# A position-wise expert mixture: 64 positions a stationary, half-width units, a block-diagonal bias product, two kinds of banks and a fetch on two queues

## The chip, the core and the metric

The kernel runs on one core of a Trainium2 chip. The metric is the device time of one execution in microseconds. The core's engines run side by side and meet through semaphores: TensorE (PE in the rows, its weight loads PEld), VectorE (DVE), ScalarE (ACT), GpSimd (POOL) and SyncE (SP, which here only issues DMAs).

## What is computed

The program is a chain of twelve stages of a perceiver over x, 32 batches of 64 positions of 256 columns, all float32: cross attention, attention and a feed-forward part, four times. The change is in the first feed-forward part, a mixture of eight experts whose gates belong to a position, not to a token. Cut to what matters:

```python
h = relu(x_normed @ gW1.T + gb1)             # per token
gate = mean_over_batch(h) @ gW2.T + gb2      # (64 positions, 8 experts)
W1 = einsum('se,eoi->soi', gate, eW1)        # a weight for each position
b1 = gate @ eb1
hid = relu(einsum('bsi,soi->bso', x_normed, W1) + b1)
W2 = einsum('se,edo->sdo', gate, eW2)
b2 = gate @ eb2
x = x + einsum('bso,sdo->bsd', hid, W2) + b2
```

The hidden width is 1024. So for each of 64 positions a 256x1024 and a 1024x256 weight are mixed from eight, and each is then applied to the 32 tokens (one per batch) of its position.

## The kernel before

x is resident in SBUF (16 tiles of 128 tokens), and its normed transpose XNT is written in the order of positions by the layernorm ahead (`layernorm_transposed`, which also issues the weight loads of the stage on SP and may run a `prepare` on GpSimd). `mixed_experts` computes the gates: two matrix products, a mean over the batch, and then, on VectorE, GB (the gates in blocks of 32 rows: four outputs by eight experts, masked so that one matmul with 32 rows mixes four outputs of every position) and GR (the gates repeated for the 32 batches, 2048 columns).

`position_experts` works through 16 units k: eight hidden blocks of 128 columns (k // 2), each for two halves of the positions (k % 2). GpSimd puts the loaded weights into expert-last order (`reorder1`, `reorder2`), TensorE turns them with transposes (T1, T2, 16 each), and the jobs of a unit are then, in TensorE's hand-written order: four mixing jobs f0 to f3 for the second weight (W2M), two first products A0 and A1 (each a bias product of four matmuls over `gates(...)` and EB1, then 32 matmuls over XNT and W1M), eight flips FL of the hidden rows, two second products Y0 and Y1 (16 matmuls over HT and W2M), and four mixing jobs g0 to g3 for the next unit's first weight (W1M). A mixing job is 16 matmuls: a stationary of 32 rows and 128 columns of the turned weight, a moving operand of 128 columns of GB (32 positions by four outputs), over four row groups of TensorE. Every job writes one of two buffers of four banks, in turn; `claim` lets job j wait until all that empties job j - 2 is done. Mixing and turning jobs are emptied half by ScalarE and half by VectorE (two copies of 512 columns each), hidden rows by ScalarE, second products by VectorE, which adds them up in Y. The turned second weight W2L has two buffers.

At the end SP stores Y for each half of the positions to DRAM, fetches it back in token order into YX, and VectorE adds it to x in four pieces.

All program semaphores that a stage has given up wait in a list; at the end of a stage, when it holds 64 or more, they are cleared and all engines meet at one more barrier.

## Time and profile before

| | |
|---|---|
| median of 3 runs | 2790.12 us (2789.54 to 2791.2) |
| profiled execution | 2791.36 us, span of its profile 2789.5 us |
| TensorE busy | 2520.1 us (90%) |
| VectorE, ScalarE, GpSimd busy | 1698.8 (61%), 1389.9 (50%), 730.5 us (26%) |
| the stage of the mixture | from 452.2 us (first turn) to 830.3 us (next stage starts) |
| the same, busy in it | TensorE 332.0, VectorE 233.8, ScalarE 181.7 us of 378 |

The profile gives start and length of every instruction; runs of equal ones stand in one row with their count and the idle time ahead of them, and what ended it. It has two entries for each float32 matmul of the program, and one for each transpose. A matmul's length includes the time in which its last columns drain, so the length of a job is read better from its start to the next job's start.

### The profile page before, as it was taken

The numbers are of one execution on the slowest core, as the hardware profiler recorded it, in microseconds if no ns is written. First come the engines' busy times: TensorE is split into PE (matmuls) and PEld (weight loads), VectorE is DVE, ScalarE is ACT, GpSimd is POOL, SyncE is SP. The second block draws the span as 40 slices with busy tenths as digits, with TensorE's granted clock in tenths as the row PEclk, the third lists the DMA queues.
The fourth block names the chain that finished last, engine by engine and source line by source line (L and its number), as shares of the span: only waits on it lengthen the run. The fifth ranks groups of instructions, "written<-read, shape, count | busy, mean of one in ns | idle before, by whom it ended". The sixth has DMA issues, their size and how long they took to land. (4 is left out here: it accounts for less than half of the span.)

```text
span 2789.5 us, 84759 instructions
## 1 busy us (share of the span) xinstructions
PE 2520.1 (90%) x36489; PEld 2137.2 (77%) x36489; DVE 1698.8 (61%) x3422; ACT 1389.9 (50%) x3486; POOL 730.5 (26%) x1078
## 2 busy tenths in 40 slices
PE   7999888999968999999998859978997878999988
PEld 6888656777756899999987658976776757999577
DVE  6877675666656433333334755658885867777663
ACT  4888324555532444444432324426885444777342
POOL 3222102212102300000001213433445525666300
PEclk9999999999989999999999969998999899999999
DMA  3110003212031100000000042334220003111000
GB/s 97 36 36 21 1 2 97 63 33 63 3 83 43 44 17 17 17 17 17 2 2 25 3 147 89 134 113 143 88 74 1 3 2 99 50 51 49 1 1 31
DMA packets 118229, 126.76 MB, mean 45 GB/s; under 512 B 10877, under 2 KB 110153, under 8 KB 117865
## 3 DMA queue, kind: packets, MB, share of 16 engines
q1 hardware_dynamic: 114024, 110.93, 12.8%
q0 software_dynamic: 3840, 10.49, 1.2%
q8 instruction: 288, 4.72, 0.7%
q14 instruction: 77, 0.62, 0.1%
HBM read 105.67 MB, written 15.73 MB: 44 GB/s over the span
## 5 line engine op out<-in xcount | busy, mean ns | idle before, releaser
L1157 ACT ACTIVATE s_ca_probs<-s_ca_scores,s_ca_neg_max 128x256 f32<-128x256 f32 x768 | 352.8, 477 | 35.5 <-DVE s_ca_neg_max L1203 26.6
L1203 DVE TENSOR_REDUCE s_ca_neg_max<-s_ca_scores 128x4 f32<-128x1024 f32 x192 | 233.6, 1218 | 46.8 <-PE s_ca_scores L1056 25.5
L2212 DVE COPY s_mx_w_mixed<-s_mx_ps 128x512 f32<-128x512 f32 x256 | 163.5, 683 | 94.9 <-PE s_mx_ps L2058 81.4
L1073 PE MATMUL s_ca_probs_flipped<-identity,s_ca_probs 128*128 128x128 f32 x1536 | 210.6, 280 | 1.7 <-ACT s_ca_probs L1157 1.7
L1073 PEld LDWEIGHTS s_ca_probs_flipped<-identity,s_ca_probs 128*128 128x128 f32 x1536 | 164.4, 141 | 40.1 <-issue 20.8
L2167 ACT COPY s_mx_w_mixed<-s_mx_ps 128x512 f32<-128x512 f32 x256 | 137.3, 589 | 107.6 <-PE s_mx_ps L2045 86.0
L1157 ACT ACTIVATION_READ_ACCUMULATOR s_ca_probs<-s_ca_scores,s_ca_neg_max 128x1 f32 x768 | 160.3, 209 | 0.0
L1164 ACT COPY s_ca_probsT<-s_ca_probs_flipped 128x512 f32<-128x512 f32 x192 | 115.2, 600 | 77.5 <-PE s_ca_probs_flipped L1073 77.5
L82 PE MATMUL s_cc_shared<-s_cc_ctxT_low,h_cc_wkv_high 128*128 128x256 f32 x512 | 145.9, 285 | 2.2 <-DVE s_cc_ctxT_low L1556 2.2
L971 POOL TENSOR_TENSOR s_ca_inv_spread<-s_ca_inv_sums,h_ca_own_half 128x128 f32<-128x128 f32 x192 | 72.6, 399 | 287.2 <-DVE s_ca_inv_sums L1225 287.1
L300 POOL TENSOR_SCALAR x_normed_transposed<-x_normed_transposed,h_cc_rstd,h_cc_shift 128x256 f32<-128x256 f32 x56 | 30.6, 556 | 447.1 <-PE s_cc_out L1450 271.4
L83 PE MATMUL s_cc_shared<-s_cc_ctxT_high,h_cc_wkv_low 128*128 128x256 f32 x512 | 144.6, 282 | 0.0
L84 PE MATMUL s_cc_shared<-s_cc_ctxT_high,h_cc_wkv_high 128*128 128x256 f32 x512 | 144.4, 282 | 0.0
L1209 DVE COPY s_ca_probsT<-s_ca_probs_flipped 128x512 f32<-128x512 f32 x192 | 130.1, 677 | 14.3 <-PE s_ca_probs_flipped L1073 14.3
L1514 ACT COPY s_cc_kT<-s_cc_shared 128x512 f32<-128x512 f32 x128 | 75.0, 586 | 117.8 <-PE s_cc_shared L84 117.8
L1570 DVE RECIPROCAL s_cc_inv_sums<-s_cc_out 128x8 f32<-128x8 f32 x32 | 6.6, 207 | 183.8 <-PE s_cc_out L1450 183.8
L82 PE MATMUL s_cc_shared<-h_cc_wkv_low,s_cc_ctxT_high 128*128 128x512 f32 x256 | 107.4, 420 | 1.7 <-issue 1.7
L1096 PE MATMUL s_ca_out<-s_ca_probsT,h_ca_v_spread 128*32 128x64 f32 x6144 | 105.7, 220 | 0.7 <-DVE s_ca_probsT L1209 0.4
L677 POOL MEMSET s_ln_eps<- 128x1 f32 x9 | 0.9, 98 | 395.4 <-POOLq L60 215.7
L1096 PEld LDWEIGHTS s_ca_out<-s_ca_probsT,h_ca_v_spread 128*32 128x32 f32 x6144 | 90.3, 110 | 17.0 <-issue 17.0
L90 PE MATMUL s_ln_flip<-identity 128*128 128x128 f32 x276 | 49.0, 359 | 58.8 <-PEq L2490 26.1
L84 PE MATMUL s_cc_shared<-h_cc_wkv_high,s_cc_ctxT_high 128*128 128x512 f32 x256 | 101.2, 395 | 0.0
(571 smaller groups left out, 7613.4 us busy)
## 6 DMA issues: line engine op xcount, KB each, us to landing
h_ca_ctxT<-in_ctxT SPq DMA_DIRECT2D x96, 256.0 KB, 3.3
h_mx_w_by_input<-in_L_ffn_eW1T SPq DMA_DIRECT2D x16, 512.0 KB, 5.5
h_mx_w_by_hidden<-in_L_ffn_eW2T SPq DMA_DIRECT2D x8, 1024.0 KB
h_re_win<-in_L_ffn_W_in SPq DMA_DIRECT2D x8, 1024.0 KB, 5.9
h_ca_ctx<-in_ctx SPq DMA_DIRECT2D x32, 256.0 KB, 2.8
x_normed_transposed<-in_ctx SPq DMA_DIRECT2D x7, 1024.0 KB, 5.3
h_re_wout<-in_L_ffn_W_out SPq DMA_DIRECT2D x8, 512.0 KB, 3.8
choice_results<-s_rt_zeros SPq DMA_DIRECT2D x4, 1024.0 KB, 10.6
```

Of the source, the lines that this page charges most:

```text
L82: nc.tensor.matmul(dst, lhs[0], rhs[1], start=start, stop=False)
L83: nc.tensor.matmul(dst, lhs[1], rhs[0], start=False, stop=False)
L84: return nc.tensor.matmul(dst, lhs[0], rhs[0], start=False, stop=stop)
L1073: last = nc.tensor.transpose(psT[u % len(psT)][:, 2 * a + c, :], PR[b % 2][:, 4 * n + 2 * h + a, c * P:(c + 1) * P], ident[:, :])
L1096: last = nc.tensor.matmul(psO[32 * r:32 * r + 32, g * SEQ:(g + 1) * SEQ], V[b % 2][:, c, g * NR + r, 2 * h:2 * h + 2, :].rearrange("p a d ...
L1157: last = nc.scalar.activation(PR[b % 2][:, p, :], psS[:, p // 2, (p % 2) * NKEY:(p % 2 + 1) * NKEY], ACT.Exp, bias=nmax[b % 2][:, p:p + 1] ...
L1164: nc.scalar.copy(PT[b % 2][:, 4 * n:4 * n + 2, :, :].rearrange("p a c q -> p (a c) q"), psT[u % len(psT)][:, :, :]).then_inc(s_ta, 1)
L1203: nc.vector.tensor_reduce(nmax[b % 2][:, 4 * n:4 * n + 4], psS[:, 2 * n:2 * n + 2, :].rearrange("p r (g k) -> p r g k", g=GR), AX_X, ALU.m ...
L1209: nc.vector.tensor_copy(PT[b % 2][:, 4 * n + 2:4 * n + 4, :, :].rearrange("p a c q -> p (a c) q"), psT[u % len(psT)][:, :, :]).then_inc(s_ ...
L1514: nc.scalar.copy(KT[:, 2 * k:2 * k + 2, :].rearrange("p m s -> p (m s)"), psA[bank(f)][:, :]).then_inc(s_empty[bank(f)], 1)
L2167: last = nc.scalar.copy(part(int(name[1]), r), bank(j, r))
L2212: last = nc.vector.tensor_copy(part(int(name[1]), r), bank(j, r))
```

## The change

- A unit is now a hidden block and a kind: two units for the two halves of the hidden columns (64 each) and two for the two halves of the output columns (128 each), with all 64 positions. There are 32 units. A mixing job has 8 matmuls of 256 columns (64 positions by four outputs); there are four a unit. The mixed weights lie in two tiles used in turn.
- A first product is 64 matmuls of 64 columns (two a unit), a second product 16 matmuls of 128 columns (four a unit), each into one bank.
- The bias product has one stationary of 32 rows (four groups of positions by eight experts, GR now 512 columns) and a block-diagonal EB1 or EB2, so that one matmul serves four groups; GpSimd clears those tiles in the layernorm ahead (`clear`).
- Mixing jobs have three pairs of banks of their own; a mixing job uses two pairs, and waits for the first copy of each engine of the job before. All small jobs (first and second products, flips, turns) use two single banks in turn. Turns and flips are emptied by ScalarE alone, in copies of 512 columns; the turned second weight has one buffer.
- The result is stored in three pieces and fetched in two halves of the columns, the first on ScalarE's queue, the second on SP's; VectorE adds most of it, GpSimd six tiles of the second half.

The diff, cut to its core:

```diff
-        self.EB1, self.EB2 = sb("mx_b1", [P, self.DFF]), sb("mx_b2", [P, DIM])
+        self.EB1, self.EB2 = sb("mx_b1", [32, 16, 4, 64]), sb("mx_b2", [32, 2, 4, P])
...
+    def clear(self, pool):
+        pool.memset(self.EB1[:, :, :, :], 0.0).then_inc(self.s_zero, 1)
+        pool.memset(self.EB2[:, :, :, :], 0.0).then_inc(self.s_zero, 1)
...
-                    nc.vector.tensor_copy(GR[:, :, :], G.unsqueeze(2).broadcast_to([P, SEQ, BATCH])).then_inc(s_o, 1)
-                    dve.wait_ge(s_o, 8)
+                    dve.wait_ge(s_o, 7)
+                    own = GB[:, :, :, :].rearrange("p k (m i q) o -> p (k m) i q o", m=2, i=4)
+                    nc.vector.tensor_tensor(G4[:, :, :], own[:, :, 0, :, 0], own[:, :, 1, :, 1], ALU.add).then_inc(s_o, 1)
...
+    def order(u):
+
+        ob, out = u // 4, []
+        mixes = [("M", u + 1, n) for n in range(NQ)] if u + 1 < NU else []
+        t1 = [("T1", ob + 1, n) for n in range(NQ)] if ob + 1 < OB else []
+        if u % 4 == 0:
+            between = [[("A", u, 0)], [("T2", ob, 0), ("T2", ob, 1)], [("A", u, 1)], [("T2", ob, 2), ("T2", ob, 3)]]
+        elif u % 4 == 1:
+            between = [[("A", u, 0)], [("A", u, 1)], [("F", u, 0), ("F", u, 1)], [("F", u, 2), ("F", u, 3)]]
+        elif u % 4 == 2:
+            between = [[("Y", u, 0), ("Y", u, 1)], t1[0:2], [("Y", u, 2), ("Y", u, 3)], t1[2:4]]
+        else:
+            between = [[("Y", u, n)] for n in range(NQ)]
+        for n in range(NQ):
+            out += mixes[n:n + 1] + between[n]
+        return out
...
+                def mix(u, n):
+
+                    ob, half, m = u // 4, u % 2, 4 * u + n
+                    if n == 0 and u % 4 == 0:
+                        pe.wait_ge(s_small_act, emptied(BY_ACT, PLACE[("T1", ob, 3)]))
+                    if n == 0 and u % 4 == 2:
+                        pe.wait_ge(s_small_act, emptied(BY_ACT, PLACE[("T2", ob, 3)]))
+                    if m >= 1:
+                        pe.wait_ge(s_mix_act, 2 * m - 1)
+                        pe.wait_ge(s_mix_dve, 2 * m - 1)
...
+                    for n in range(2):
+                        nc.tensor.matmul(dst[:, n * 256:(n + 1) * 256], GR[0:32, 2 * h + n, :, :].rearrange("p q b -> p (q b)"),
+                                         EB1[:, u // 4 * 2 + u % 2, :, :].rearrange("p i o -> p (i o)"), start=(n == 0), stop=False)
...
+                act.wait_ge(s_back[0], 16)
+                fetch(act, 0, slice(0, SEQ))
...
-                layernorm_transposed(nc, X, XNT, ident, ST, by_position=True, loads=(g, w))
+                layernorm_transposed(nc, X, XNT, ident, ST, by_position=True, loads=(g, w), prepare=w.clear)
```

Two places show how the instructions moved. The first is TensorE at the start of the first hidden block, before: s_mx_ps is either of the two buffers; L2058 and L2045 are mixing, L2074 the bias product, L2081 the first product, L2032 turns, L2090 flips.

```order
L2058 MATMUL s_mx_ps<-me_gate_blocks,s_mx_w_1 128x128 x16
L2074 MATMUL s_mx_ps<-h_mx_b_1,me_gate_rows 128x128 x4
L2081 MATMUL s_mx_ps<-s_mx_w_mixed,x_normed_transposed 32x128 x32
L2058 MATMUL s_mx_ps<-me_gate_blocks,s_mx_w_1 128x128 x16
L2032 MATMUL s_mx_ps<-identity,h_mx_w_expert_last 128x128 x16
L2058 MATMUL s_mx_ps<-me_gate_blocks,s_mx_w_1 128x128 x16
L2074 MATMUL s_mx_ps<-h_mx_b_1,me_gate_rows 128x128 x4
L2081 MATMUL s_mx_ps<-s_mx_w_mixed,x_normed_transposed 32x128 x32
L2058 MATMUL s_mx_ps<-me_gate_blocks,s_mx_w_1 128x128 x16
L2090 MATMUL s_mx_ps<-identity,s_mx_hidden 128x128 x8
```

The same place after the change: L2041 is mixing, L2062 the bias product, L2068 the first product, L2113 turns of the second weight.

```order
L2041 MATMUL s_mx_mix_ps<-me_gate_blocks,s_mx_w_1 128x256 x40
L2062 MATMUL s_mx_small_ps<-h_mx_b_1,me_gate_rows 128x256 x2
L2068 MATMUL s_mx_small_ps<-s_mx_mixed,x_normed_transposed 32x64 x64
L2041 MATMUL s_mx_mix_ps<-me_gate_blocks,s_mx_w_1 128x256 x8
L2113 MATMUL s_mx_small_ps<-identity,h_mx_w_expert_last 128x128 x8
L2041 MATMUL s_mx_mix_ps<-me_gate_blocks,s_mx_w_1 128x256 x8
L2062 MATMUL s_mx_small_ps<-h_mx_b_1,me_gate_rows 128x256 x2
L2068 MATMUL s_mx_small_ps<-s_mx_mixed,x_normed_transposed 32x64 x64
L2041 MATMUL s_mx_mix_ps<-me_gate_blocks,s_mx_w_1 128x256 x8
L2113 MATMUL s_mx_small_ps<-identity,h_mx_w_expert_last 128x128 x8
L2041 MATMUL s_mx_mix_ps<-me_gate_blocks,s_mx_w_1 128x256 x8
```

Mixing jobs have half as many matmuls of twice the columns, the bias product two instead of four, the first product 64 of half the width; the second weight's turns come in two lots, and the mixing job in the last row is the first that reads what they turn.

The second place is ScalarE in the same unit, before: it empties half of each mixing and turning job (L2167, L2159) and the hidden rows (L2173).

```order
L2173 ACTIVATE s_mx_hidden<-s_mx_ps 128x512
L2167 COPY s_mx_w_mixed<-s_mx_ps 128x4x32x4 x2
L2159 COPY s_mx_w_2<-s_mx_ps 128x512 x2
L2167 COPY s_mx_w_mixed<-s_mx_ps 128x4x32x4 x2
L2173 ACTIVATE s_mx_hidden<-s_mx_ps 128x512
```

And after, where L2142 empties mixing, L2163 the turned second weight and L2148 the hidden rows.

```order
L2148 ACTIVATE s_mx_hidden<-s_mx_small_ps 128x8x64
L2142 COPY s_mx_mixed<-s_mx_mix_ps 128x2x64x4 x2
L2163 COPY s_mx_w_1<-s_mx_small_ps 128x512 x2
L2142 COPY s_mx_mixed<-s_mx_mix_ps 128x2x64x4 x2
L2148 ACTIVATE s_mx_hidden<-s_mx_small_ps 128x8x64
L2142 COPY s_mx_mixed<-s_mx_mix_ps 128x2x64x4 x2
L2163 COPY s_mx_w_1<-s_mx_small_ps 128x512 x2
L2142 COPY s_mx_mixed<-s_mx_mix_ps 128x2x64x4 x2
```

ScalarE has all of a turn's copies now, behind the two copies of the mixing job ahead of it.

## Rows read from the trace of the kernel before

**Rows 1.** One stretch: length, busy us (entries) of PE, PEld, DVE, ACT, POOL; granted clock, DMA.

```profile
605.00:650.00 45.00, 41.62 (x988) 33.24 (x987) 28.73 (x44) 22.84 (x43) 7.67 (x3) 1.00 0.17 49
```

**Rows 2.** TensorE's order of time: start us, us, engine, line, operation, count, idle before.

```profile
557.33 1.97 PE L2032 MATMUL s_mx_ps<-identity,h_mx_w_expert_last 128*128 128x128 f32 x16
...
602.37 1.97 PE L2032 MATMUL s_mx_ps<-identity,h_mx_w_expert_last 128*128 128x128 f32 x16
604.26 1.17 PE L2058 MATMUL s_mx_ps<-me_gate_blocks,s_mx_w 32*128 32x128 f32 x32
605.80 0.50 PE L2074 MATMUL s_mx_ps<-h_mx_b,me_gate_rows 8*128 8x128 f32 x8 [0.37 <-DVE s_mx_w L2204]
606.24 1.96 PE L2081 MATMUL s_mx_ps<-s_mx_w_mixed,x_normed_transposed 128*32 128x128 f32 x64
608.12 1.17 PE L2058 MATMUL s_mx_ps<-me_gate_blocks,s_mx_w 32*128 32x128 f32 x32
609.23 1.09 PE L2090 MATMUL s_mx_ps<-identity,s_mx_hidden 128*128 128x128 f32 x8
...
611.90 1.93 PE L2107 MATMUL s_mx_ps<-s_mx_w_mixed,s_mx_hiddenT 128*32 128x256 f32 x32
613.76 1.17 PE L2045 MATMUL s_mx_ps<-me_gate_blocks,s_mx_w 32*128 32x128 f32 x32
```

**Rows 3.** TensorE's order of time in the first cross attention.

```profile
100.71 1.10 PE L1096 MATMUL s_ca_out<-s_ca_probsT,h_ca_v_spread 128*32 128x64 f32 x64
101.74 1.09 PE L1073 MATMUL s_ca_probs_flipped<-identity,s_ca_probs 128*128 128x128 f32 x8
...
104.19 1.15 PE L1056 MATMUL s_ca_scores<-s_ca_kT,s_ca_q_spread 32*128 32x256 f32 x16
105.27 1.09 PE L1073 MATMUL s_ca_probs_flipped<-identity,s_ca_probs 128*128 128x128 f32 x8
```

**Rows 4.** A group of the whole trace (busy us, mean ns), and two rows in time.

```profile
L2697 PE MATMUL s_vt_ps<-h_vt_w,x_normed_transposed 128*128 128x256 f32 x64 | 14.1, 380 | 1.0 <-PEq L779 1.0
...
479.74 0.71 PE L2102 MATMUL s_mx_ps<-h_mx_b,me_gate_rows 8*128 8x256 f32 x8 [0.24 <-DVE s_mx_y L2226]
480.38 1.93 PE L2107 MATMUL s_mx_ps<-s_mx_w_mixed,s_mx_hiddenT 128*32 128x256 f32 x32
```

**Rows 5.** The two copy engines in time, after a mixing job.

```profile
609.36 1.07 ACT L2167 COPY s_mx_w_mixed<-s_mx_ps 128x512 f32<-128x512 f32 x2 [0.51 <-PE s_mx_ps L2058]
...
L2212 DVE COPY s_mx_w_mixed<-s_mx_ps x256: 678/680/693, 457.1 to 807.0; 128x512 f32<-128x512 f32 x128
```

**Rows 6.** The start of the mixture in time.

```profile
449.38 2.28 DVE L1916 COPY me_gate_rows<-s_mg_psg 128x2048 f32<-128x2048 f32 x1
...
452.20 3.68 PE L2032 MATMUL s_mx_ps<-identity,h_mx_w_expert_last 128*128 128x128 f32 x32 [0.83 <-PEq L1862]
...
462.68 0.50 PE L2074 MATMUL s_mx_ps<-h_mx_b,me_gate_rows 8*128 8x128 f32 x8 [0.34 <-DVE s_mx_w_mixed L2212]
```

**Rows 7.** The end of the mixture in time (SPq: a DMA being issued).

```profile
812.11 1.22 DVE L2228 TENSOR_TENSOR s_mx_y<-s_mx_ps,s_mx_y 128x1024 f32<-128x1024 f32 x1 [0.50 <-PE s_mx_ps L2107]
813.36 0.38 SPq L1982 DMA_DIRECT2D me_rows_by_position<-s_mx_y  x1
817.84 1.22 SPq L1989 DMA_DIRECT2D s_mx_w_mixed<-me_rows_by_position  x2
825.14 4.63 DVE L2254 TENSOR_TENSOR x_resident<-x_resident,s_mx_w_mixed 128x1024 f32<-128x1024 f32 x4 [11.81 <-DMA s_mx_w_mixed<-me_rows_by_position]
830.30 5.32 DVE L686 BATCH_NORM_STATS2 x_statistics<-x_resident 128x6 f32<-128x256 f32 x16 [0.53 <-PEq L1976]
```

**Rows 8.** A stage boundary with a clear of semaphores, in time.

```profile
414.95 0.43 DVE L1815 BATCH_NORM_STATS2 x_statistics<-x_resident 128x6 f32<-128x256 f32 x1
416.78 0.19 DVE L688 TENSOR_TENSOR s_ln_square_sum<-x_statistics 128x16 f32<-128x16 f32 x1 [1.40 <-PEq L60]
```

**Rows 9.** A clear of 2048 columns on GpSimd: ns min/median/max, first and last start.

```profile
L2686 POOL MEMSET l1a_v<- x4: 1804/1804/1805, 1525.0 to 1530.2; 128x2048 f32 x4
```

More of the change, by code:

```diff
@@ L1929, in position_experts @@
     OB = DFF // P
[L1930 removed]
+    NU = 4 * OB
+    NQ = 4
     GS = 4
[L1932 to L1942 removed]
@@ L1944, in position_experts @@
-    JOBS = [(0, "T1"), (0, "T2")] + [(0, f"g{n}") for n in range(4)]
-    for k in range(NK):
-        JOBS += [ahead(k, n) for n in ORDER if ahead(k, n)[0] < NK]
-    PLACE = {kn: j for j, kn in enumerate(JOBS)}
-    def job(k, name):
-        return PLACE[(k, name)]
-    def emptied(users, j):
-        return sum(n in users for _, n in JOBS[:j + 1])
-    def name_of(j):
-        return JOBS[j][1]
-    back = nc.dram_tensor("me_rows_by_position", (SEQ * BATCH, DIM), F32, kind="Internal").ap()
+    OH, DH = P // 2, DIM // 2
@@ L1961, in position_experts, with emptied @@
+    SMALL = [("T1", 0, n) for n in range(NQ)] + [j for u in range(NU) for j in order(u) if j[0] != "M"]
+    PLACE = {j: n for n, j in enumerate(SMALL)}
+    BY_ACT, BY_DVE = ("A", "F", "T1", "T2"), ("Y",)
+    def emptied(users, n):
+        return sum(j[0] in users for j in SMALL[:n + 1])
+    back = nc.dram_tensor("me_rows_by_position", (2, SEQ * BATCH, DH), F32, kind="Internal").ap()
     with stage(nc) as (sb, ps, sem):
-        W1L = sb("mx_w1", [P, 8, DIM])
-        W2L = [sb("mx_w2", [P, 16, P]) for _ in range(2)]
@@ L1976, in position_experts, with mixed1, mixed2, fetch @@
+        def mixed1(u):
+            return MIXED[u % 2][:, :].rearrange("p (c s o) -> p c s o", c=KC, s=SEQ)
+        def mixed2(u):
+            return MIXED[u % 2][:, :].rearrange("p (s d) -> p s d", s=SEQ)
+        def fetch(queue, h, rows):
+            got = back[h].rearrange("(s t b) n -> b s t n", b=2, t=TILES)
+            for b in range(2):
+                queue.dma_start(YX[b * SEQ + rows.start:b * SEQ + rows.stop, :, h * DH:(h + 1) * DH], got[b, rows]).then_inc(s_here[h], 16)
         with nc.Block() as block:
@@ L1995, in _ @@
                     held.load2(sp, ob)
+                sp.wait_ge(s_small_dve, emptied(BY_DVE, PLACE[("Y", NU - 2, 3)]))
+                store(0, slice(0, SEQ), 0)
                 for h in range(2):
-                    store(h)
-                    fetch(h)
+                    sp.wait_ge(s_small_dve, emptied(BY_DVE, PLACE[("Y", NU - 1, 2 * h + 1)]))
+                    store(1, slice(32 * h, 32 * h + 32), h + 1)
+                for h in range(2):
+                    sp.wait_ge(s_back[h + 1], 16)
+                    fetch(sp, 1, slice(32 * h, 32 * h + 32))
```

428 lines of the change are left out of this document (176 added, 252 removed).

## The prediction

> **What bounds the kernel now.** I read four views in this order: busy time in a stretch, TensorE's order of time with what ended its idle time, the copies' times, then the edges of the stage. The stretch row [rows 1] shows TensorE busy 41.6 of 45 us in the expert mixture, at granted clock 1.00 (2.4 GHz), VectorE 28.7 and ScalarE 22.8: the stage is bound by TensorE's own work, and what is left for a better order is 3.4 us in 45. The order of time [rows 2] shows the work. A hidden block (128 hidden columns of all eight experts; there are eight) takes 602.37 - 557.33 = 45.04 us. I take lengths from one start to the next: a mixing job 1.11 (608.12 to 609.23), the first layer's bias product 0.44, its product 1.88, a second product 1.86 (611.90 to 613.76), sixteen turning transposes 1.89, eight flips about 1.0. A block has 16 mixing jobs (17.8), four first products with bias (9.3), four second products (7.4), 32 turns (3.8) and 16 flips (2.0): 40.3. The other 4.7 are waits for a bank to be emptied, as the 0.37 ahead of the bias product, and the drains ahead of them.
>
> **Mixing jobs.** Each now issues 8 matmuls of 256 columns instead of 16 of 128, on the same four row groups; the trace counts a float32 matmul twice, so 16 instead of 32. The columns that pass are the same. The cross attention of this kernel has that form, 32 rows and 256 columns on four row groups: 16 of them take 1.08 (104.19 to 105.27, [rows 3]). So half the stationaries give 1.11 - 1.08 = 0.03 a job, 0.5 a block. The work is the passing of columns, not the number of loads.
>
> **First products.** They are 128 instructions of 64 columns where 64 of 128 columns stood. The same form in the cross attention takes 1.03 for 64 [rows 3], against 1.88 for 64 at 128 columns: 0.85 goes with the columns, 0.18 is fixed. That makes 0.18 + 1.70 = 1.88 for the new job; twice 1.03, 2.06, is the other end. I take 1.90.
>
> **Bias product.** Before, eight instructions lie on four row groups, so four run side by side: 0.44 at 128 columns [rows 2], and 0.64 at 256 columns in the second layer (479.74 to 480.38, [rows 4]). A round of 128 columns is thus worth about 0.10, and 0.24 is fixed. The block-diagonal product has all its 32 rows in one row group: its four instructions of 256 columns follow each other, 4 x 0.20 + 0.24 = 1.05. Whole-array matmuls of 256 columns, one behind another, take 14.1/64 = 0.22 each [rows 4], so 0.88 is the low end; 1.15 the high one. With the product that is 2.95 a job against 2.32: +0.63, +2.5 a block. In the first block the second layer's bias does the same at 512 columns: eight jobs of 2 x 0.40 + 0.24 = 1.05, 8.4, against 4 x 0.64 = 2.6: +5.8 once.
>
> **Second products, turns, flips.** Two pairs of second products at 1.86 and four single ones at 1.0 (half of 1.71, and 0.15 fixed) make 7.7 against 7.4. Turns and flips stand as six pairs of 8 transposes at 1.0: 6.0 against 5.8. Work of a block: 17.3 + 11.8 + 7.7 + 6.0 = 42.8, 2.5 more than before.
>
> **The waits.** Mixing no longer shares two buffers with everything else: a mixing job waits only for the first of each engine's two copies of the job before. The copies start 609.36 - (608.12 + 1.17) = 0.07 after the mixing job's end [rows 2, 5]; with VectorE's 0.68 [rows 5] and 0.13 for the release (an estimate) its first copy is there after 0.9, and the small job between takes 1.0 or more: covered, with 0.1 to spare. If that cover fails, up to ten places a block wait some 0.1. What is not covered: the last pair of turns of each weight stands directly ahead of the first mixing job that reads it, and ScalarE alone empties turns, behind the two copies of the mixing job before. Two copies take 1.07 [rows 5], so the second starts 0.48 after the first; four in a row end 3 x 0.48 + 0.59 = 2.05 after they begin, so the turned weight is ready some 2.3 after the mixing job ended, and the pair of turns covers 1.0 of it. That is 1.3, twice a block: 2.6, with 0.1 for the rest 2.7, against 4.7 before. Before, the turned second weight had two buffers and a whole unit of time. Behind this wait TensorE's whole queue stands. A block: 42.8 + 2.7 = 45.5 against 45.04, +0.5, over eight +3.7.
>
> **Start and end of the loop.** Before, the first bias product comes 462.68 - 452.20 = 10.5 after the first turn [rows 6]. Now four turn jobs are emptied by ScalarE alone, two banks in turn (0.47 of turning, 0.59 of copy and 0.2 of releases each, some 3.0 in all), then four mixing jobs have nothing between them and wait for the first copies (1.08 + 0.9 each, 8.0), and a fifth follows (1.1): 12.1, +1.6. The second weight's turns, done by then before, are still to come, and the last block, which had no turns left, keeps them: 2.0 + 0.5. The last unit's second products wait for the last mixed copies with nothing beside them: about +1. The loop: 3.7 + 5.8 + 1.6 + 2.5 + 1 = +14.6.
>
> **Outside the loop.** The gate copy of 2048 columns, 2.28 [rows 6], becomes three adds of 16 columns (0.19 each, [rows 8]) and a copy of 512 (0.7): -1.0 at most, I take -0.7. At the end, from the last result (812.11 + 1.22 = 813.33) to the next stage (830.30) there are 17.0 [rows 7]: store 4.5, fetch 7.3, adds 4.6, the rest the boundary. Now only a quarter of the result is stored last (512 KB: 2.5 to 4.5), half a megabyte fetched (4 to 7.3), and VectorE adds 1280 columns (1.5); the other half's fetch runs just before on the same DMA engines. I take 13 for 17: -4, with -6 and 0 as bounds. The stage has seven more semaphores, so pending ones reach the limit of 64 in other places: clears stand at seven stage boundaries instead of six. A boundary with a clear takes 416.78 - 415.38 = 1.4 [rows 8], one without 0.53 [rows 7]: +0.9. Clearing the bias tiles on GpSimd is 5120 columns, 4.5 by [rows 9], begun when the layernorm ahead of the mixture starts (416.78, [rows 8]); the bias loads behind it are first read at 462.68 [rows 6], 46 us later. Without that cover it would cost its 4.5.
>
> **The sum.** +14.6 - 0.7 - 4 + 0.9 = +10.8 on the profiled execution's 2791.36 (span 2789.5); that execution is 1.2 above the median of 2790.12, so the forecast is 2801.
>
> **Where a rule weighs against a row.** The main page of the Trainium skill, Trainium Kernel Development and Optimization (Key Constraints), says that DMAs issued from several engines' queues run on the same 16 DMA engines, so that a second queue saves only issue time: by it the fetch on two queues gives nothing beyond the smaller pieces, and with the end at -1 the sum would be 2804. No row of before shows two queues fetching at once.
>
> **The rivals.** First, loads of stationaries are exposed in each round of mixing, so that halving them counts. In [rows 2] a job of eight rounds takes 1.11, of which 8 x 0.107 would be columns; the remaining 0.26 would be 0.032 a round, four rounds fewer save 0.13, and 128 jobs 16.6 instead of the 3.8 that I counted: 2788. With the bias at its low end (32 x 0.17 = 5.4) it is 2783, faster. It decides from a mixing job under 0.96. Against it: the cross attention's burst of the very form [rows 3]. TensorE: Matmul & The Clock Gate (Part 3, The mechanism), of the Trainium skill, has the rule for it: a load overlaps matmuls in flight only in other row groups. Second, on the slow side, the 0.1 to spare at the mixing claims is not there: ten waits of 0.15 a block, 12 us, 2813; it decides as soon as a copy's release takes 0.1 longer than I reckoned. Third, the work is right but the bias is cheap (0.88, -5.4) and the end gains its full 6: 2794, no change. That the two-queue fetch does nothing is the 2804 above, by the row of the store: 4.5 for a megabyte whichever queue.
>
> **How the numbers follow.** A measurement of this kernel can tell about 0.2% (5.6 us) from no change. Forecast, 2796 to 2808: 0.46. Second rival, above that: 0.18. Between 2784.5 and 2795.7, the third rival and most of the first: 0.22. Faster: 0.14. So slower 0.64. The range takes the mixing job between 1.00 and 1.11 (-10 to +4), the bias ends (-5 to +3), 2.06 for the first product (+5) and the thin covers (+12), which do not all fall together: 2786 to 2818.
>
> **What would show it.** Right: mixing bursts of 16 at 1.05 to 1.10; bias bursts of four near 1.05, not 0.44; a wait of about 1.3 for ScalarE's turned copy ahead of the first mixing job of each weight; a block of 45.5; first half's fetch on the ACT queue, and 13 us from the last result to the next stage. Wrong: mixing bursts under 0.96, or waits at every mixing claim, or a block under 44.

## The result and the profile after

| | before | after |
|---|---|---|
| median | 2789.83 us (4 runs, 2789.09 to 2791.2) | 2829.78 us (4 runs, 2825.72 to 2831.24) |
| ratio, 95% interval | | 1.0134 (1.012 to 1.0148) |
| profiled execution, span | 2791.36, 2789.5 | 2829.4, 2827.3 |
| TensorE's entries, matmuls | 36,489 | 37,369 |

The change costs 40 us, where 11 were forecast. The spans differ by 37.8. Set side by side, the two traces show where (the last row's forecast is one more clear of semaphores):

| stretch | before | after | difference | forecast |
|---|---|---|---|---|
| up to the first turn of the mixture | 452.20 | 453.80 | +1.6 | -0.7 |
| first turn to last result | 361.13 | 386.06 | +24.9 | +14.6 |
| last result to the next stage | 16.97 | 16.67 | -0.3 | -4 |
| all stages behind the mixture | 1959.2 | 1970.8 | +11.6 | +0.9 |

**The loop.** TensorE's order of time in the changed kernel, one stretch with nothing in its way but the wait for a turned weight, answers to [rows 2]:

```profile
622.85 1.15 PE L2041 MATMUL s_mx_mix_ps<-me_gate_blocks,s_mx_w 32*128 32x256 f32 x16
623.92 1.09 PE L2113 MATMUL s_mx_small_ps<-identity,h_mx_w_expert_last 128*128 128x128 f32 x8
626.16 1.15 PE L2041 MATMUL s_mx_mix_ps<-me_gate_blocks,s_mx_w 32*128 32x256 f32 x16 [1.15 <-ACT s_mx_w L2163]
627.13 1.02 PE L2062 MATMUL s_mx_small_ps<-h_mx_b,me_gate_rows 32*128 32x256 f32 x4
628.08 1.99 PE L2068 MATMUL s_mx_small_ps<-s_mx_mixed,x_normed_transposed 128*32 128x64 f32 x128
630.01 1.15 PE L2041 MATMUL s_mx_mix_ps<-me_gate_blocks,s_mx_w 32*128 32x256 f32 x16
```

From start to start: mixing 1.07, bias 0.95, first product 1.93, and 1.15 of waiting for ScalarE's turned copy. Those are the forecast's own numbers to within 0.15. But the waits of the whole stage (column: us in total, times, longest) have a kind that [rows 2] hardly knows:

```profile
PE s_mx_mix_ps L2041 <- ACT s_mx_w L2163: 9.2, 8, 1.1
PE s_mx_mix_ps L2041 <- ACT s_mx_w L2158: 8.7, 8, 1.1
PE s_mx_small_ps L2068 <- issue: 4.7, 3, 2.5
PE s_mx_mix_ps L2041 <- DVE s_mx_mixed L2182: 4.5, 5, 0.9
PE s_mx_mix_ps L2041 <- issue: 2.7, 2, 2.1
```

"issue" is idle time in which TensorE waits for nothing that the profile shows; below it is called idle time without a cause. In pauses of 0.25 us and more it is 8.5 us in the mixture and 10.1 behind it; before the change it was 0.3 and 3.7, and the mixture had one such pause:

```profile
PE s_mx_ps L2058 <- issue: 0.3, 1, 0.3
```

One pause of the changed kernel with what stands around it, in order of time:

```profile
581.03 0.37 SPq L354 DMA_DIRECT2D h_mx_w_by_hidden<-in_L_ffn_eW2T  x1
582.38 1.15 PE L2041 MATMUL s_mx_mix_ps<-me_gate_blocks,s_mx_w 32*128 32x256 f32 x16
583.35 1.02 PE L2062 MATMUL s_mx_small_ps<-h_mx_b,me_gate_rows 32*128 32x256 f32 x4
584.30 1.55 PE L2068 MATMUL s_mx_small_ps<-s_mx_mixed,x_normed_transposed 128*32 128x64 f32 x96
587.78 0.65 PE L2068 MATMUL s_mx_small_ps<-s_mx_mixed,x_normed_transposed 128*32 128x64 f32 x32 [1.94 <-issue]
```

It lies inside one job, between two matmuls of the same kind, so no semaphore stands there. The DMA view of the stretch 578 to 592 (busy tenths of the 16 engines in 40 slices; packets, MB and share by queue):

```profile
DMA  0002000000006899999971000000000100000000
q1 hardware_dynamic: 1040, 1.05, 22.1%
q8 instruction: 3, 0.05, 1.5%
```

The full slices are the megabyte of the second weights, from 582 to 586. Queue 8 carries instructions: 295 packets of 16 KB in the whole run, for 37,369 matmuls and as many weight loads, so some 253 a packet. (The run with half columns alone, number 6 below, has 4,096 matmuls and loads more than the kernel before and 304 packets for 288: 256 each.) A first product of 64-column matmuls has 128 matmuls and 128 loads: it uses up one packet in 1.92 us; before, with 128-column matmuls, it was half a packet in 1.88 [rows 2]. The trace's packets on that queue in the stage start no closer than 3.45 us to each other (before: 3.45). Here one starts at 579.28, the next only at 585.38, when the load is nearly through, and TensorE goes on 2.4 us later.

The other pauses end in the same way. In the fourteen traces of this case the mixture has 142 pauses of this kind, and 141 of them end 2.2 to 2.9 us after a packet on that queue has started; of all matmuls of the loop in the changed kernel only 15% start at such a distance from a packet. Behind the mixture it is so for 12 of the changed kernel's 14 pauses (8.9 of 10.1 us) and 4 of 6 before (2.4 of 3.7).

**The end.** Last results, the two queues' transfers and the additions, in order of time, against [rows 7]:

```profile
833.36 6.99 SPq L2006 DMA_DIRECT2D me_rows_by_position<-s_mx_y  x3
...
838.66 1.94 ACTq L1998 DMA_DIRECT2D s_mx_mixed<-me_rows_by_position  x2
839.17 0.69 DVE L2192 TENSOR_TENSOR s_mx_y<-s_mx_small_ps,s_mx_y 128x512 f32<-128x512 f32 x1 [0.18 <-PE s_mx_small_ps L2094]
841.98 7.08 SPq L1998 DMA_DIRECT2D s_mx_mixed<-me_rows_by_position  x4
...
852.90 1.49 DVE L2204 TENSOR_TENSOR x_resident<-x_resident,s_mx_mixed 128x1280 f32<-128x1280 f32 x1 [1.07 <-DMA s_mx_mixed<-me_rows_by_position]
852.95 3.10 POOL L2215 TENSOR_TENSOR x_resident<-x_resident,s_mx_mixed 128x768 f32<-128x768 f32 x1 [83.34 <-DMA s_mx_mixed<-me_rows_by_position]
```

The last store, of half a megabyte, is issued at 839.89 and lands at 847.83: 7.9 us, where a whole megabyte took 4.4 before. ScalarE's megabyte moves beside it; run 12 tests whether that is why. GpSimd's addition, twice as long as VectorE's, ends last, at 856.05, 1.7 later than VectorE's.

**Ahead of the mixture.** The clears of the bias tiles run on GpSimd beside the layernorm, and VectorE stands:

```profile
417.43 3.50 POOL L366 MEMSET h_mx_b<- 32x4096 f32 x1
418.06 0.18 DVE L698 TENSOR_TENSOR s_ln_mean_sum<-x_statistics 128x16 f32<-128x16 f32 x1
418.28 2.69 DVE L699 TENSOR_SCALAR s_ln_mean<-s_ln_mean_sum 128x16 f32<-128x16 f32 x1
421.00 0.25 DVE L710 RECIPROCAL s_ln_rstd<-s_ln_std 128x16 f32<-128x16 f32 x1
```

The operation at 418.28 took 0.17 before; it ends with the clear. Of these 2.5 us nothing is left at the start of the gates, whose first matmul comes 0.7 later than before, as the layernorm did: VectorE's own idle time at that boundary is 4.0 us, where it was 6.0. In the gates TensorE's granted clock is at its half level (1.2 GHz) for 6.8 us (before: 3.4), and their first product takes 1.5 longer; the cheaper gate copy gives back 0.5. The Trainium skill (SBUF — State Buffer, Who interferes with whom) says that such an operation can contend with GpSimd for a shared pair of ports, and that whoever issues first has the pair for its whole instruction while the other is blocked; the row agrees with it.

**Theories for the experiments.** Mine: the missing 27 us (37.8 between the spans, 10.8 forecast) are TensorE's supply of instructions (in the mixture, and behind it through where the later code lies in its packets of 256), the end's transfers in each other's way, and semaphore clears that moved. The rivals: the new order with its waits, the load of the weights as such, or the clears alone.

### The profile page after: what moved, and what is told of

It reads as the page before. It is cut to its first block and busy times, and to the rows that moved or that the text cites. A ratio compares the mean times of both kernels' runs of the same rounds, so it can differ in the third digit from the quotient of the medians.

```text
span 2827.3 us, 86644 instructions
## 1 busy us (share of the span) xinstructions
PE 2545.4 (90%) x37369; PEld 2148.6 (76%) x37369; DVE 1678.7 (59%) x3407; ACT 1414.8 (50%) x3534; POOL 738.7 (26%) x1081
## 3 DMA queue, kind: packets, MB, share of 16 engines
q10 hardware_dynamic: 2080, 1.05, 0.1%
## 5 line engine op out<-in xcount | busy, mean ns | idle before, releaser
L2182 DVE COPY s_mx_mixed<-s_mx_mix_ps 128x512 f32<-128x512 f32 x256 | 165.0, 686 | 173.2 <-PE s_mx_mix_ps L2041 173.2
L2142 ACT COPY s_mx_mixed<-s_mx_mix_ps 128x512 f32<-128x512 f32 x256 | 137.5, 589 | 114.4 <-PE s_mx_mix_ps L2041 113.1
L2041 PE MATMUL s_mx_mix_ps<-me_gate_blocks,s_mx_w 32*128 32x256 f32 x2048 | 149.6, 402 | 25.2 <-ACT s_mx_w L2163 9.2
L2041 PEld LDWEIGHTS s_mx_mix_ps<-me_gate_blocks,s_mx_w 32*128 32x128 f32 x2048 | 94.1, 185 | 51.7 <-issue 19.1
```

The source lines that it names most:

```text
L2041: last = nc.tensor.matmul(PAIR[(2 * m + r // 2) % 3][:, r % 2, q * 256:(q + 1) * 256], w, GB[rows, :, :, :].rearrange("p k s o -> p (k s o ...
L2142: nc.scalar.copy(part(u, n, r), bank(u, n, r)).then_inc(s_mix_act, 1)
L2182: nc.vector.tensor_copy(part(u, n, r), bank(u, n, r)).then_inc(s_mix_dve, 1)
```

## The experiments

The changed kernel has the four runs above and was not run again beside the experiments; the kernel before was, with medians from 2789.83 to 2792.96. Differences of some 3 us between medians of different sets are therefore not told apart from none.

**1 and 2: what was lost behind the mixture.** The kernel before, with six unused semaphores, or with 48 instructions that only wait, behind TensorE's last work of the mixture:

```diff
+        for n in range(6):
+            sem(f"unused{n}")
```

```diff
+                for _ in range(96):
+                    pe.wait_ge(s_b, 128)
```

(Two waits go into one instruction.)

> The kernel before with six semaphores more in the mixture stage, which nothing uses: the semaphore clears then close the stages 5, 10, 15, 19, 22, 27 and 31 as in the changed kernel, and not 5, 11, 16, 20, 23 and 28; nothing else changes. Theory (the changed kernel lost some 11 us behind the mixture, and the moved clears are only a small part): one clear more at 1.4 us and a little of TensorE's clock at the new places, 2791 to 2793 us. Rival (the moved clears are what the stages behind lost): 2797 to 2801 us.

Measured: 2795.27 against 2791.01, ratio 1.0018 (1.0009 to 1.0028), +4.3: between the theory's range and the rival's, so neither.

> The kernel before with 48 instructions on TensorE behind its last work in the mixture that only wait for a semaphore that has long come, in a stretch in which TensorE is idle for 18 us. All later code of TensorE then stands 48 instructions further on, which is what the changed kernel's 1,840 more instructions come to when whole packets of 256 (16 KB, the size of the packets on the instruction queue) are taken off. Theory (the idle time for which the profile shows no cause, 10.1 us behind the mixture after the change and 3.7 us before, is TensorE waiting for its next packet of instructions, and where it falls depends on where the code stands in its packets): that idle time rises to 8 to 11 us in this kernel, at the head products of the second cross attention, and the time to 2793 to 2798 us. Rival (it comes from elsewhere, as from the clears or the transfers): 2789 to 2791 us, and the idle time stays under 5 us.

Measured: 2793.59, ratio 1.0012 (1.0002 to 1.0021), +2.6, at the low end of the theory. Idle time without a cause behind the mixture is 5.9 us, short of the 8 to 11 expected, but at the place expected, the head products of the second cross attention:

```profile
PE s_cc_scores L1436 <- issue: 4.5, 10, 1.1
```

In the changed kernel, and then in the kernel before:

```profile
PE s_cc_scores L1442 <- issue: 5.9, 10, 1.3
PE s_cc_scores L1436 <- issue: 1.0, 3, 0.5
```

How much later than in the kernel before a stage's ScalarE and VectorE operations start, as growth over three stretches (times of before) and over all behind the mixture:

| profiled execution | 1200 to 1480 | 1870 to 1930 | 2590 to 2670 | all |
|---|---|---|---|---|
| changed kernel | +4.5 | +2.2 | +3.0 | +11.4 |
| six semaphores | -0.2 | +2.1 | +3.0 | +4.3 |
| 48 instructions | +3.2 | -0.4 | 0.0 | -1.6 |

The edits bring back the changed kernel's losses place by place: the code's place the first, the moved clears the other two. The last is the head of the recurrent gate, which a clear now precedes; TensorE there, with the clear's barrier as the releaser, in the run with six semaphores:

```profile
2608.29 3.75 PE L3499 MATMUL s_gr_psz<-x_normed_transposed,h_gr_w 128*128 128x512 f32 x4 [3.56 <-PEq L60]
...
2621.58 1.19 PE L3499 MATMUL s_gr_psz<-x_normed_transposed,h_gr_w 128*128 128x512 f32 x1 [3.13 <-DVE s_gr_input L3574]
```

In the kernel before:

```profile
2606.55 2.84 PE L3497 MATMUL s_gr_psz<-x_normed_transposed,h_gr_w 128*128 128x512 f32 x4 [2.07 <-PEq L927]
...
2615.77 1.96 PE L3497 MATMUL s_gr_psz<-x_normed_transposed,h_gr_w 128*128 128x512 f32 x4 [0.42 <-DVE s_gr_input L3572]
```

So a clear costs more than its 1.4 [rows 8] where a second pause follows the first. Single executions scatter by several us behind the mixture (the profiled one with 48 instructions was the fastest of its ten), so the medians carry the verdict and the table only the places.

**3: both together.**

> The kernel before with both edits of the first two runs: six semaphores more, so that the clears close the stages at which they stand in the changed kernel, and 48 waiting instructions on TensorE behind the mixture's work, so that later code lies in its packets as in the changed kernel. The mixture itself is the kernel before's. Theory (the 11.5 us that the changed kernel lost behind the mixture are these two, and they add): 4 and 3 us, 2797 to 2800 us. Rival A (together they cost what was lost, 11 us, since a stall also lets the clock fall at the clears): 2801 to 2804 us. Rival B (they don't add, since one hides behind the other): 2793 to 2796 us, and most of what was lost behind the mixture has another cause.

Measured: 2803.82 against 2790.63, ratio 1.0044 (1.003 to 1.0058), +8 to +16: rival A, and as much as was lost. The two runs alone add 6.8 together. Its profiled execution loses 12.8 us behind the mixture, 6.2 of them at the recurrent gate, but only 1.4 in the stretch of the cross attention, with 3.6 us of idle time without a cause, as little as before. So the two edits are enough for the loss; how it divides between them in a given execution stays open, and that the wait for instructions is what the loss behind the mixture consists of is not shown: here the loss came without it.

**4: fewer clears**, in the kernel before (the limit of pending semaphores at which they are cleared):

```diff
-PENDING = 64
+PENDING = 120
```

> The kernel before with the clears of semaphores put off until 120 are waiting, not 64: three clears, which close the stages 9, 18 and 24, in place of six. Theory (a clear with its barrier costs 1.4 us and more where it keeps TensorE idle ahead of a stage): 4 to 8 us less than the kernel before, 2782 to 2786 us. Rival (a clear of twice as many semaphores takes twice as long, or it hides behind the loads of the next stage): within 2 us of the kernel before.

Measured: 2787.09 against 2791.26, ratio 0.9985 (0.9975 to 0.9996). Three clears less save 4.2 us, the low end of the theory's 4 to 8: the version that beats both kernels, if by little.

**5: the load out of the way.**

```diff
                     sp.wait_ge(s_r2, ob)
+                    if ob > 1:
+                        sp.wait_ge(s_small, PLACE[("F", 4 * (ob - 2) + 1, 3)] + 1)
                     held.load2(sp, ob)
```

> The changed kernel with the load of the second weights (1 MB) held back until the flips of the running block are done, so that it moves under second products and turns and no longer under first products. Theory (TensorE's stalls of 1.94, 0.60 and 2.50 us in the mixture are instruction packets that stood behind that load while the first products use up instructions fastest): the idle time without a cause in the mixture falls from 8.5 us to under 4, TensorE's clock stays up through the stage, and the time falls by 4 to 8 us to 2822 to 2826 us. Rival (the stalls have nothing to do with that load): within 2 us of the changed kernel, 2828 to 2832 us.

Measured: 2822.63, 7.2 below the changed kernel. Idle time without a cause in the mixture is 4.5 for 8.5 (under 4 was expected). In the profiled execution the loop is 4.3 us shorter than the changed kernel's; 5.9 more were gained behind the mixture, where this edit changes nothing of the work, so of the 7.2 only some 4 are shown to be the load's. The clock, which was to stay up, falls once in the loop, for 3.4 us at 534, as it fell at 727 in the changed kernel, behind its pause of 2.5. The pause of 1.94 at 587.78 is 0.25 now, that of 2.50 is 0.30:

```profile
584.38 1.55 PE L2070 MATMUL s_mx_small_ps<-s_mx_mixed,x_normed_transposed 128*32 128x64 f32 x96
586.18 0.65 PE L2070 MATMUL s_mx_small_ps<-s_mx_mixed,x_normed_transposed 128*32 128x64 f32 x32 [0.25 <-issue]
```

The theory holds for these two. Of what is left, 2.15 us stand in the start, beside the first weights' load; the pause of 0.60, at 635 in the changed kernel, stayed as it was with no load beside it: the supply is short there by itself.

**6: half columns alone**, in the kernel before:

```diff
                     for j in range(4):
-                        for c in range(KC):
-                            for q in range(GS):
+                        for o in (slice(0, 64), slice(64, P)):
+                            for c in range(KC):
+                                for q in range(GS):
...
-                                last = nc.tensor.matmul(dst[32 * q:32 * q + 32, j, 0:P], XNT[:, c, at:at + BATCH],
-                                                        W1M[:, c, s, :], ...)
+                                    last = nc.tensor.matmul(dst[32 * q:32 * q + 32, j, o], XNT[:, c, at:at + BATCH],
+                                                            W1M[:, c, s, o], ...)
```

> The kernel before with each product of 128 columns in the first products done as two of 64 columns, and nothing else changed: 2,048 products more in the trace, and as many weight loads; later code keeps its place in the packets. Theory (instruction supply): the products themselves cost 3 to 4 us more (66.3 against 62.9 us busy), a first product takes 256 instructions in 2 us where it took 128, and TensorE is idle without a cause for 5 to 20 us in the mixture; 2800 to 2815 us. Rival (the stalls in the changed kernel come from its order and its loads and not from the half columns): under 2 us of idle time, 2793 to 2797 us.

Measured: 2817.7 against 2792.96, ratio 1.0094 (1.0077 to 1.0111), +24.7. All of it lies in the mixture: the next stage starts at 856.02 instead of 830.30, and all that follows adds 1.1 (the edit adds 16 whole packets, so that later code lies as before). Order, bias, banks and loads are the kernel before's. TensorE in time:

```profile
607.25 1.65 PE L2082 MATMUL s_mx_ps<-s_mx_w_mixed,x_normed_transposed 128*32 128x64 f32 x103
610.41 0.55 PE L2082 MATMUL s_mx_ps<-s_mx_w_mixed,x_normed_transposed 128*32 128x64 f32 x25 [1.51 <-issue]
610.89 1.17 PE L2058 MATMUL s_mx_ps<-me_gate_blocks,s_mx_w 32*128 32x128 f32 x32
612.00 1.97 PE L2032 MATMUL s_mx_ps<-identity,h_mx_w_expert_last 128*128 128x128 f32 x16
613.89 1.17 PE L2058 MATMUL s_mx_ps<-me_gate_blocks,s_mx_w 32*128 32x128 f32 x32
615.43 0.50 PE L2074 MATMUL s_mx_ps<-h_mx_b,me_gate_rows 8*128 8x128 f32 x8 [0.37 <-DVE s_mx_w L2205]
615.87 1.99 PE L2082 MATMUL s_mx_ps<-s_mx_w_mixed,x_normed_transposed 128*32 128x64 f32 x128
617.79 0.71 PE L2058 MATMUL s_mx_ps<-me_gate_blocks,s_mx_w 32*128 32x128 f32 x13
619.22 0.93 PE L2058 MATMUL s_mx_ps<-me_gate_blocks,s_mx_w 32*128 32x128 f32 x19 [0.71 <-issue]
```

An undisturbed first product takes 1.92, 0.04 more than with whole columns, which is 1.3 us over 32 of them, where the theory had 3 to 4. Of the rest 19.6 us are idle time without a cause, all of it in pauses that end 2.2 to 2.9 us after a packet, and in 15 of the 19 no load moved ahead of that packet; the time is above the theory's range. This settles it for the mixture: twice the instructions for the same columns is enough to leave TensorE waiting.

**7: the waits for the turned weights.**

```diff
-            between = [[("A", u, 0)], [("T2", ob, 0), ("T2", ob, 1)], [("A", u, 1)], [("T2", ob, 2), ("T2", ob, 3)]]
+            between = [[("T2", ob, 0), ("T2", ob, 1)], [("A", u, 0)], [("T2", ob, 2), ("T2", ob, 3)], [("A", u, 1)]]
...
-            between = [[("Y", u, 0), ("Y", u, 1)], t1[0:2], [("Y", u, 2), ("Y", u, 3)], t1[2:4]]
+            between = [t1[0:2], [("Y", u, 0), ("Y", u, 1)], t1[2:4], [("Y", u, 2), ("Y", u, 3)]]
```

> The changed kernel with the turns one place earlier in their units: each pair of turns ahead of the first or second product that it stood behind, so that a product of 1.9 us stands between the last turns and the mixing that waits for their copies. Theory (as in the prediction, 16 waits of 1.15 us for the copies of turned weights): the waits at the turned weights fall from 18 us to under 3 us and the time by 13 to 18 us, to 2812 to 2817 us. Rival (the time then shows elsewhere, since the copies of the mixed weights or of the small jobs come later): less than 5 us is gained, 2825 us or more.

Measured: 2814.11, 15.7 below the changed kernel, as in the theory (14.0 in the loops of the two traces, with idle time without a cause at 8.9 for 8.5); of the sixteen waits one is left, 0.7 at the start. The forecast's wait was real, and another order takes it away at no cost elsewhere.

**8: the bias products side by side.** With EB1 also on rows 32 to 63, and, unlike run 7, all four second turns of a unit ahead of its two first products (the core of the edit; what it replaces is left out):

```diff
+                        both = (dst, claim(("A", u, 1)))
+                        for n in range(2):
+                            for a in range(2):
+                                rows = slice(32 * a, 32 * a + 32)
+                                nc.tensor.matmul(both[a][:, n * 256:(n + 1) * 256], GR[rows, 2 * a + n, :, :]...,
+                                                 EB1[rows, u // 4 * 2 + u % 2, :, :]..., start=(n == 0), stop=False)
```

> The changed kernel with the turns as early as in the run with early turns (both pairs of second turns even ahead of both first products), and the bias products of a unit's two first products issued together ahead of the first, one on rows 0 to 31 for one bank and one on rows 32 to 63 for the other, so that they can run beside each other. Theory (a bias product of 0.95 us before each of 32 first products runs alone on a quarter of the array; side by side two cost little more than one): four matrix products of bias take 1.0 to 1.2 us instead of twice 0.95, 16 times 0.7 to 0.9 us less than the early turns alone, 2799 to 2804 us. Rival (the bias is bound by its columns whatever the rows, or the second bank is claimed too early and TensorE waits for it): 2811 to 2817 us, as with the early turns alone.

Measured: 2833.56, 19.5 above the early turns alone, though the pairs do what was expected:

```profile
628.76 1.03 PE L2066 MATMUL s_mx_small_ps<-h_mx_b,me_gate_rows 32*128 32x256 f32 x8
629.72 0.58 PE L2072 MATMUL s_mx_small_ps<-s_mx_mixed,x_normed_transposed 128*32 128x64 f32 x25
630.61 1.66 PE L2072 MATMUL s_mx_small_ps<-s_mx_mixed,x_normed_transposed 128*32 128x64 f32 x103 [0.32 <-issue]
632.20 1.15 PE L2042 MATMUL s_mx_mix_ps<-me_gate_blocks,s_mx_w 32*128 32x256 f32 x16
633.27 0.32 PE L2072 MATMUL s_mx_small_ps<-s_mx_mixed,x_normed_transposed 128*32 128x64 f32 x8
634.46 1.88 PE L2072 MATMUL s_mx_small_ps<-s_mx_mixed,x_normed_transposed 128*32 128x64 f32 x120 [0.87 <-issue]
```

Two bias products take 0.96 together instead of 1.90, 15 us less work, and the idle time without a cause in the mixture rises to 23.8 us, 15 more than with the early turns. The granted clock, moreover, is at its half level for 13.7 us at the start and 10 more in the loop (early turns: 6.8 in all), which by an estimate, half of the difference, costs 8 to 9 us more. The stretch at the start need not belong to this edit: run 12, whose start is the changed kernel's, has one of 17.1 us there. Both theories missed: the gain was real and was taken away elsewhere.

**9 to 11: all of it, the same in another order, and shifted.**

> The changed kernel with what the runs so far point to: early turns and paired bias products, the second weights' load held behind the flips (and the first weights' second load too), clears only from 120 semaphores on, and 13 of 16 blocks of the last addition on VectorE, not 10. Theory (the causes found add up): 2829.8 less 16 for the turns, 12 for the bias, 8 for the loads, 5 for the clears and 1 for the addition, 2785 to 2793 us, within 0.2% of the kernel before. Rival (they overlap, since stalls of instruction supply come back where TensorE runs faster): 2796 us or more.

Measured: 2808.85. The rival was right: 15.7 us of idle time without a cause.

The other order (first products of a unit first, then the turns; the mixing waits for the half it reads):

```diff
-            between = [[("T2", ob, 0), ("T2", ob, 1)], [("T2", ob, 2), ("T2", ob, 3)], [("A", u, 0)], [("A", u, 1)]]
+            between = [[("A", u, 0)], [("A", u, 1)], [("T2", ob, 0), ("T2", ob, 1)], [("T2", ob, 2), ("T2", ob, 3)]]
...
+                    if n == 0:
+                        pe.wait_ge(s_small_act, emptied(BY_ACT, PLACE[("T1" if u % 4 < 2 else "T2", ob, 2 * half + 1)]))
```

> The run of all changes together with the same work in another order: the two pairs of second turns stand between the first products of one unit and those of the next, and no longer ahead of all four, so that never more than two first products follow each other; so that the mixing need not wait for the last turns, it waits only for the half of the turned weights that it reads. Theory (TensorE's instructions come in packets of 256 no closer than 3.3 to 3.6 us, and a first product of 64-column products uses up 256 in 1.9 us, so that four in a row outrun the supply): the idle time without a cause in the mixture falls from 17 us to under 6, and the time by 8 to 13 us to 2796 to 2801 us. Rival (the stalls follow the faster bias or the fewer waits and not the order): more than 12 us of them stay, 2805 us or more.

Measured: 2805.22; the idle time stays at 15.8: the rival. My theory fell in this form: four in a row are not needed. Counted in entries (matmuls and loads) and in the start-to-start times of undisturbed jobs, a stretch asks for a packet of 256 every so many us:

| stretch | entries | us | us a packet |
|---|---|---|---|
| before: mixing, bias, first product [rows 2] | 64 + 16 + 128 | 3.86 | 4.75 |
| changed kernel: the same, 626.16 to 630.01 | 32 + 8 + 256 | 3.85 | 3.3 |
| half columns alone | 64 + 16 + 256 | 3.9 | 3.0 |
| paired bias: two mixings, two first products | 64 + 16 + 512 | 6.96 | 3.0 |

The closest two packets of a run start 3.2 to 3.5 us apart, in each of the fourteen traces. Set beside the table: before, there was room; the changed kernel is at the limit, and 6.6 of its 8.5 us of pauses stand behind the first or second weights' load; the last two are beyond it. That the distance of packets is a fixed limit is argued from these traces and not tested by itself. What is shown is that the cheaper bias product was paid back in waiting in both orders tried.

> The same with 192 instructions on TensorE behind its last work in the mixture that only wait for a semaphore that has long come, so that all later code stands in its packets of 256 where it stands in the kernel before. Theory (the stalls behind the mixture depend on where the code lies in its packets): the idle time without a cause behind the mixture falls from 6 to 9 us to under 5, and the time by 2 to 4 us against the run without the shift. Rival: less than 1 us.

Measured: 2806.42, no gain. The idle time behind the mixture fell from 7.6 to 4.1 as expected, but the time did not: the 192 instructions were not hidden as the 48 had been; the next stage starts 21.4 us after the last result, 17.9 without them.

**12: the end.**

```diff
-                store(0, slice(0, SEQ), 0)
...
-                act.wait_ge(s_back[0], 16)
-                fetch(act, 0, slice(0, SEQ))
```

> The changed kernel with the way of the first half of the result's columns through memory left out (its store and its fetch; the sum takes the rows as they lie, so the first 128 columns of this output are not the layer's). Theory (the end takes 16.7 us and not 13 because 1 MB of fetch moves beside the last store, which took 7.9 us, and beside the last fetches): the last store falls to 4 to 5 us, the last fetch to 4 to 5 us, the end from the last result to the next stage to 11 to 13 us, and the time by 3 to 6 us to 2824 to 2827 us. Rival (the end is bound by its chain of store, fetch and the addition on GpSimd and not by what moves beside it): the end stays at 16 us or more, and the time within 1.5 us of the changed kernel.

Measured: the last store issued at 840.60 lands at 843.85 (3.3 for 7.9), and the end takes 12.3 us instead of 16.7:

```profile
839.88 0.69 DVE L2189 TENSOR_TENSOR s_mx_y<-s_mx_small_ps,s_mx_y 128x512 f32<-128x512 f32 x1 [0.18 <-PE s_mx_small_ps L2093]
842.09 2.98 SPq L1998 DMA_DIRECT2D s_mx_mixed<-me_rows_by_position  x4
849.25 1.49 DVE L2201 TENSOR_TENSOR x_resident<-x_resident,s_mx_mixed 128x1280 f32<-128x1280 f32 x1 [6.35 <-DMA s_mx_mixed<-me_rows_by_position]
852.88 0.36 SPq L677 DMA_DIRECT2D s_ln_col<-in_L_xattn_ln_l_w_col  x1
```

The last store fell by more than in the theory and the end as in it; the time did not: 2827.45, 2.3 below the changed kernel, within the scatter of either. In the profiled execution TensorE's clock was at its half level for 17.1 us from 457 on, and the loop took 388.7 us instead of 386.1; so the trace's end decides. The Trainium skill (DMA: Bandwidth & Descriptors, Issuing engines are not separate DMA queues) says that transfers of all queues share the same engines and interleave; the store at 7.9 beside the other fetch and 3.3 without it agree.

## Why the prediction was wrong

The step that failed is the pricing of the first products: by their columns alone, with TensorE's supply of instructions nowhere in the sum. The work of the loop came out almost as summed; what it lacked are 11 us in which TensorE stood, or ran late, around pauses that end once a packet of instructions has come. Two more steps failed: the stages behind the mixture, priced at one more clear (0.9), lost 11.6, and the end, forecast 4 shorter, came out 0.3 shorter. That it got slower at all was forecast for a reason that held: the loop without its lateness is 13.8 us longer, forecast 14.6.

- **Mixing jobs** (1.08): right, 1.07 to 1.08. The first rival, that halving the stationaries counts, fell.
- **First products** (1.90): right as work, 1.92. Here they were costed as columns, and the bounds (1.88 to 2.06) came from a burst of 64 in the cross attention [rows 3]. That burst is half as long, so it does not ask for a packet in 2 us. Twice the entries for the same columns was on the page as a count and never set against the rate at which instructions come.
- **Bias** (1.05): 0.95, near the low end. In the first block's second layer 0.95 as well: 8 x 0.95 - 2.6, +5.0, forecast +5.8.
- **Waits for the turned weights** (1.3 each): right, 1.15, and removing them gave 15.7 of the 19 that sixteen of them with their drains came to. **Thin cover**: held; mixing waits for copies only at the start and the end, 4.5 us, and where it does it waits 0.9, so that the 0.13 for a copy's release, an estimate without a row of its own, was near. The second rival fell.
- **A block** (45.5 against 45.04): from one block's first bias product to the next one's, the two blocks without a pause take 45.03 and 45.18, all six behind the first 46.6 in the mean; the same six before take 44.65 in the mean, 45.04 the longest. So the growth of 0.5 was right, with luck in it: the start and the result were both some 0.4 too long. **Start** (12.1): 12.2.
- **The loop** (+14.6): +24.9. The start takes 1.8 more than before (forecast 1.6), the first block 8.3 (6.3), the next six 11.4 (2.8), the rest 3.5 (4.0). The excess is in the blocks with pauses: 11.1 us over their undisturbed times, of which 8.5 are idle time without a cause and the rest drains around it and 3.4 us at half clock. Without that the loop is +13.8.
- **The end** (-4): -0.3. I had both queues' transfers in mind and kept the store at 2.5 to 4.5; it took 7.9. And the sum had VectorE's last addition (1.5, measured 1.49) but not GpSimd's six tiles beside it, which took 3.1 and ended last. The sentence by the rule of the Trainium skill, -1, was nearer. **The third rival**, with the bias cheap and the end at its full gain, had the bias half right and the end wrong.
- **Gate copy** (-0.7): -0.5. **The clears of the bias tiles** (hidden for 46 us): hidden, though not as foreseen: VectorE stood 2.5 us, and its idle time at the stage's boundary took up most of that. The half clock in the gates was not foreseen.
- **One more clear** (+0.9): six unused semaphores, which move the clears as the change does, cost 4.3, with growth at two of the places where clears now stand; and nothing in the prediction stood for the place of later code in its packets (+2.6 alone). Both edits together cost 8 to 16, as much as was lost there; in what share, and by what at each place, is open.

Of the 27 us between the spans that were missing, 10 are the loop (11.1 of lateness, less 0.8 of work that was over-forecast), 4 the end, 11 the stages behind, 2 those ahead. The loop's share is shown by a run that makes such pauses in the kernel before (half columns alone) and one that unmakes some (the later load), the end's by the run without the first half; the share behind is shown as the sum of two edits and not part by part.

## To carry to other kernels

Count instructions as well as columns. In this case TensorE hardly waited where a stretch asked for 256 entries every 4.75 us, waited mostly behind loads at 3.3, and again and again at 3.0; there 15 us of saved bias work came back as idle time without a cause, while the saved waits of run 7 stayed saved. Where such a job runs, keep large loads away from it, or give it fewer and longer matmuls. A changed count of semaphores or instructions moves clears and code for all that follows; before small differences are put down to an edit, look at the stages behind it.

## What was not expected of the hardware

- The profile lists TensorE's instructions among the transfers of the 16 DMA engines, in packets of 16 KB on a queue of their own, 3.2 us apart at the closest in any of these runs. Where a 1 MB load moved at up to 390 GB/s, the next packet started only when it was nearly through, and in the longest of these pauses TensorE stood for 1.9 to 3.0 us.
- The Trainium skill (Runtime: NRT & Kernel Launch, Instruction fetch mechanics) describes the refill in blocks of 16 KiB, 256 instructions, by a queue of the sequencer's own, and calls the cost mostly hidden, since instructions are dispatched more slowly than they are filled in. The packets' size agrees. That it is hidden holds for the kernel before (0.3 us in the mixture) and not with 64-column matmuls (8.5 and 19.6 us): the measurement decides.
- A clear of semaphores at one more boundary cost 1.4 us there and up to 3 at the head of the recurrent gate, where the clock was at its half level for 6.8 and 3.4 us (before: 3.4 once).
